# Order of the max units and the value product inside a step of the unmasked attentions of a two-layer decoder

## The chip, the cores and the metric

The kernel runs on one core of one Trainium2 chip. The metric is the device time in microseconds (us) of one execution; lower is better. The core has five engines with instruction streams of their own, which meet only at semaphores: TensorE (PE in the profile, its weight loads PEld), VectorE (DVE), ScalarE (ACT), GpSimd (POOL) and SyncE (SP, which issues DMAs here).

## The reference: what is computed

The input is 2048 tokens of 256 features, with a context of 1601 tokens. Two decoder layers follow one another. Each has a causal self-attention, a cross-attention to the context, and a feed-forward part, each followed by a layer norm. There are thus four attentions of 16 heads of 16 features each:

1. layer 0, self-attention, causal (2048 x 2048 scores a head), with rotary positions;
2. layer 0, cross-attention with a mask on the keys (2048 x 1601);
3. layer 1, self-attention, causal;
4. layer 1, cross-attention without a mask (2048 x 1601).

Each computes `softmax(q k^T / 4) v` for every head, then a product with an output matrix. The last part of layer 1 is a mixture of eight experts with a shared one.

## The kernel before, in words

All four attentions are built by one function, `attention_phase` (L103). A **head** is worked off in **steps**, which are listed in `slots`: a step is one tile of 128 keys (`kt`) against one half (1024) of the queries. Cross-attention has 26 steps a head (13 key tiles, two halves). Causal attention has 24 (16 key tiles; the first half of the queries has no part in key tiles 8 to 15, and the further down the diagonal, the fewer the columns). The last field of a slot says whether it is the second half of its key tile, which is where the product with the values stands.

Scores are computed transposed (keys in the rows of PSUM, queries in its columns), and ACT takes their exponential. So the maximum of each query has to be known before, and it is got from a second computation of the same scores, the other way round: the **units** (`unit`, PE at L541, DVE at L725). One unit is 128 queries against up to 512 keys. PE makes it with four matmuls side by side (L555), each in a quarter of the array's columns and in one half of its rows: `g % 2` picks the half for unit number g. It writes one of **three** PSUM banks (`M_BANKS = 3`), bank `g % 3`. DVE reads the bank and reduces it to 128 maxima: `tensor_reduce` (L747) for whole units, a fused add and maximum with the triangular mask (L734) for a unit that ends on the diagonal, and in attention 4 one reduction over four narrow units at once (L745). The PE's wait ahead of a unit is the one that matters here:

```python
                    if g >= M_BANKS:
                        pe.wait_ge(unit_used, g - M_BANKS + 1)
```

Unit g may thus be issued only when DVE has finished unit g - 3. A causal head has 40 units, the cross-attention of layer 1 has 52 (four of them of 4 x 65 columns).

The other kinds of PE work in a step are:

- `scores(h, n)` (L559): the scores of slot n with the maxima already subtracted. There are two PSUM areas for them (`S_PS`), so it waits until ACT has finished the slot two before. The columns of the first bank use the lower half of the array's rows, those of the second bank the upper half. L576 is its matmul; in attention 1 a crossing of the diagonal adds four short ones (L582).
- `product(h, n)` (L599): probabilities of one key tile times the values, for all queries, only in steps of the second half. Its matmuls (L616) are float32 and use all 128 rows of the array. It waits for the exponentials of slot n (and in attention 3 for a selection on POOL, L439).

ACT makes one exponential a step (L480) of up to 1024 columns, and once a head copies the output out (L453).

The units of head h + 1 (for late steps those of head h + 2) are spread over the steps of head h in proportion to the step's columns: `share[n]` and `before[n]`. A step gets 0 to 3 units in a causal head and exactly 2 in attention 4. The loop at L668 to L684 then writes PE's order by hand. For step n it is: scores of step n + 2; the first half of the step's units (rounded up); in attention 2 alone the mask products; the value product if the step has one; and the rest of the units. Nothing else in the kernel sets the order of these. DVE takes the units in the same order 0, 1, 2, ... whatever stands between them, with the five small steps of `finish_max` (L749) between the first units of a head.

Of the kernel before, what the change touches and what calls it, by code (L numbers as in the profile page):

```python
# [102 lines left out]
def attention_phase(nc, e, keys, causal, masked, loads, query, key, value, ahead, projection, normed, eps, kept=None,  # L103
# [12 lines left out]
    slots = []  # L116
# [9 lines left out]
    for t in range(NT):  # L126
        cut = tiles((t + 1) * P, CH) if causal else tiles(keys, -(-keys // -(-keys // CH)))
        if wide and t % 4 == 0:
            units += [(t + j, i, a, CH, False, 1) for j in range(4) for i, (a, _) in enumerate(tiles(keys, CH)[:-1])]
            units.append((t, keys // CH, keys // CH * CH, keys % CH, False, 4))  # L130
        elif not wide:
            units += [(t, i, a, w, causal and a + w == (t + 1) * P, 1) for i, (a, w) in enumerate(cut)]
# [28 lines left out]
    with ExitStack() as held, phase(nc) as sem:  # L161
# [91 lines left out]
        with nc.Block() as block:  # L253
# [255 lines left out]
            def _(pe):  # L509
# [31 lines left out]
                def unit(h, u):  # L541


                    t, piece, a, w, diagonal, count = units[u]
                    g, b = h * nu + u, h % 3
                    if u == 0:
                        pe.wait_ge(stack_in[b], 192 * (h // 3 + 1))
                    if g >= M_BANKS:
                        pe.wait_ge(unit_used, g - M_BANKS + 1)
                    bank, first = e.ps[:, g % M_BANKS, :], g % 2 * ROWS  # L550
                    rows = slice(first, first + KQ)
                    for i in range(count):
                        for j in range(4):
                            at = (t + i) * P + 32 * j
                            last = nc.tensor.matmul(bank[quarter(j), i * w:i * w + w], qs[b][rows, at:at + 32],  # L555
                                                    ks[b][rows, a:a + w], start=True, stop=True)
                    last.then_inc(unit_ready, 1)

                def scores(h, n):  # L559

                    kt, rows, half, first, diagonal, _ = slots[n]
                    diagonal = diagonal and not select
                    g, b = h * ns + n, h % 3
                    if n == 0:
                        pe.wait_ge(max_in, 32 * (h + 1))
                    if g >= 2:
                        pe.wait_ge(exp_done, g - 1)
                    groups = -(-rows // 32)
                    for bank in range(2):
                        lo, hi = max(first, bank * CH), (bank + 1) * CH  # L570
                        if lo >= hi:
                            continue
                        crossed = diagonal and lo == first
                        at = bank * ROWS
                        for j in range(groups):
                            last = nc.tensor.matmul(S_PS(g)[quarter(j), lo:hi], ks[b][at:at + KM, kt * P + 32 * j:kt * P + 32 * j + 32],  # L576
                                                    qs[b][at:at + KM, half * HALF + lo:half * HALF + hi],
                                                    start=True, stop=not (crossed or masked))
                        if crossed:
                            for j in range(groups):  # L580
                                own = at + 32 * (j % 2)
                                last = nc.tensor.matmul(S_PS(g)[quarter(j), lo:lo + P], e.ident16[at:at + ROWS, own:own + 32],  # L582
                                                        e.lower16[at:at + ROWS, j // 2, :], start=False, stop=True)
                    if not masked:
                        last.then_inc(s_ready, 1)

                def mask_scores(h, n):

                    kt, rows, half, first, diagonal, _ = slots[n]
                    g = h * ns + n  # L590
                    for bank in range(2):
                        lo, hi = bank * CH, (bank + 1) * CH
                        for j in range(-(-rows // 32)):
                            last = nc.tensor.matmul(S_PS(g)[quarter(j), lo:hi], e.big16[0:rows, quarter(j)],  # L594
                                                    e.mask_one[0:rows, kt, half * HALF + lo:half * HALF + hi],
                                                    start=False, stop=True)
                    last.then_inc(s_ready, 1)

                def product(h, n):  # L599

                    kt, rows, _, _, _, _ = slots[n]
                    tile = h * nk + kt
                    pe.wait_ge(exp_done, h * ns + n + 1)
                    if select:
                        pe.wait_ge(selected, tile + 1)
                    if kt == 0 and h:
                        pe.wait_ge(o_copied, h)
                    if tile == 0 and v_bias:
                        pe.wait_ge(v_shifted, nk)
                    weights = e.prob[tile % P_SLOTS].rearrange("p (b j q) -> p b j q", j=4, q=P)  # L610
                    for j in range(4):
                        b0 = max(0, -(-(kt - j) // 4)) if causal else 0
                        if b0 == 4:
                            continue
                        end = kt == (12 + j if causal else nk - 1)
                        last = nc.tensor.matmul(O_PS[quarter(j, HD + 1), b0 * P:CH], e.values[0:rows, kt, h, :],  # L616
                                                weights[0:rows, b0:4, j, :], start=(kt == 0), stop=end)
                    last.then_inc(pv_done, 1)
# [49 lines left out]
                for h in range(H):  # L668
                    for n in range(ns):
                        if n + 2 < ns:  # L670
                            scores(h, n + 2)
                        elif h + 1 < H:
                            scores(h + 1, n + 2 - ns)
                        turned = h + (1 if n <= turn else 2)
                        now = range(before[n], share[n]) if turned < H else range(0)
                        middle = -(-len(now) // 2)
                        for u in now[:middle]:
                            unit(turned, u)
                        if masked and h * ns + n + 2 < H * ns:
                            mask_scores(h + (n + 2) // ns, (n + 2) % ns)  # L680
                        if slots[n][5]:
                            product(h, n)
                        for u in now[middle:]:
                            unit(turned, u)  # L684
# [1604 lines left out]
```

## Time and profile before

| | |
|---|---|
| median of 3 runs | 2954.4 us (2951.17 to 2958.16) |
| the profiled execution, its own time | 2952.49 us |
| span in its trace | 2950.7 us |
| mean granted TensorE clock | 0.963 of full speed |
| PE busy | 2762.6 us (94%) |
| DVE busy | 2153.8 us (73%) |
| ACT busy | 1821.0 us (62%) |
| POOL busy | 544.2 us (18%) |

The span runs from the first to the last instruction; 1.8 us of the profiled execution lie around it. In the span, the steps of attention 1 run from about 142 to 533 us, those of attention 2 (masked) from about 634 to 1292, those of attention 3 from about 1453 to 1840, and those of attention 4 from about 2063 to 2579; the stretches between are projections, norms and feed-forward parts, and the experts stand at the end. Matmuls are pipelined, so a PE that is shown as busy need not be at its peak, and the recorded length of a matmul is longer than the time until the next one in the same place can start.

### The profile page before, as it was taken

How to read it: one execution, taken by the hardware profiler on the slowest of the kernel's cores; microseconds unless marked ns; L12 is line 12 of the kernel's file. 1: busy time of each engine (PE TensorE's matmuls, PEld its weight loads, DVE VectorE, ACT ScalarE, POOL GpSimd, SP SyncE). 2: the span in 40 equal slices, each digit the busy share in tenths (PEclk: the TensorE clock that was granted, in tenths of full speed). 3: DMA queues.
4: the chain of work that ended last, by engine and by line, in shares of the span. 5: the costliest groups of instructions: out<-in, count | busy, mean ns of one | idle time of the engine just before them, and what ended most of it. 6: DMA issues, size and time to landing. Idle time of an engine off the chain costs nothing. (4 is left out here: it accounts for less than half of the span.)

```text
span 2950.7 us, 93752 instructions
## 1 busy us (share of the span) xinstructions
PE 2762.6 (94%) x39186; PEld 1026.9 (35%) x39187; DVE 2153.8 (73%) x5870; ACT 1821.0 (62%) x2158; POOL 544.2 (18%) x760
## 2 busy tenths in 40 slices
PE   4999999999999999985999999999999999999997
PEld 2633332522222222232322222563222222266664
DVE  7699997488888888837799996327999999561115
ACT  2278888537777777763388888322888888922222
POOL 0188880120000000001222212301100000002330
PEclk7899999979999999996899999998999999999999
DMA  3345451311000110110211112202112221121112
GB/s 98 118 116 139 128 127 48 113 29 26 26 17 24 26 27 22 24 26 31 79 41 42 42 43 50 67 2 85 26 54 54 75 60 34 36 71 58 44 43 88
DMA packets 120405, 166.78 MB, mean 57 GB/s; under 512 B 38227, under 2 KB 89310, under 8 KB 119984
## 3 DMA queue, kind: packets, MB, share of 16 engines
q1 hardware_dynamic: 102192, 117.21, 14.8%
q0 software_dynamic: 12320, 43.02, 4.8%
q8 instruction: 310, 5.08, 0.7%
q10 hardware_dynamic: 5472, 0.56, 0.2%
q14 instruction: 111, 0.91, 0.1%
HBM read 126.51 MB, written 26.72 MB: 52 GB/s over the span
## 5 line engine op out<-in xcount | busy, mean ns | idle before, releaser
L747 DVE TENSOR_REDUCE mpart<-ps 128x1 f32<-128x512 f32 x1536 | 979.1, 684 | 77.9 <-PE ps L555 74.5
L555 PE MATMUL ps<-stack 48*32 48x512 f16 (+6 forms) x13312 | 947.4, 350 | 39.5 <-DVE mpart L747 13.6
L480 ACT ACTIVATE xT<-ps,exp_scale 128x1024 f32<-128x1024 f32 (+3 forms) x800 | 794.1, 1029 | 256.4 <-PE ps L594 122.9
L480 ACT ACTIVATE cn<-ps,exp_scale 128x1024 f32<-128x1024 f32 (+4 forms) x800 | 742.2, 960 | 193.6 <-PE ps L594 92.7
L576 PE MATMUL ps<-stack 50*32 50x512 f16 (+3 forms) x11648 | 747.7, 372 | 29.4 <-ACT xT L480 22.1
L555 PEld LDWEIGHTS ps<-stack 48*32 48x32 f16 x13312 | 281.9, 90 | 1018.1 <-DVE mpart L747 515.0
L740 DVE CUSTOM_DVE_ANT_0 scrap<-ps,arena 128x401 bf16<-128x401 f32 (+1 forms) x1024 | 533.8, 574 | 121.8 <-PE ps L555 121.8
L616 PE MATMUL ps<-xT,vall 128*17 128x512 f32 (+4 forms) x3648 | 411.0, 511 | 2.7 <-POOL xT L439 1.7
L616 PE MATMUL ps<-cn,vall 128*17 128x512 f32 (+3 forms) x3392 | 406.3, 500 | 1.3 <-ACT cn L480 1.0
L734 DVE CUSTOM_DVE_ANT_0 scrap<-ps,scrap 128x128 bf16<-128x128 f32 (+3 forms) x512 | 247.3, 484 | 14.9 <-PE ps L555 9.8
L594 PE MATMUL ps<-arena,big 128*32 128x512 fp8e4 (+1 forms) x3264 | 256.7, 386 | 0.0
L576 PEld LDWEIGHTS ps<-stack 50*32 50x32 f16 x11648 | 186.5, 89 | 175.9 <-ACT xT L480 94.2
L1681 PE MATMUL ps<-arena,vall 128*128 x312 | 146.6, 593 | 0.6 <-ACT vall L1755 0.6
L1938 DVE TENSOR_TENSOR vall<-osb,ps 128x512 f32<-128x512 f32 x39 | 26.8, 688 | 146.0 <-PE ps L1681 146.0
L1771 ACT ACTIVATE osb<-ps 128x512 f32<-128x512 f32 x39 | 23.3, 598 | 169.8 <-PE ps L1681 169.8
L1162 POOL PARTITION_ALL_REDUCE small<-small x1 | 0.4, 373 | 679.5 <-issue 679.5
L616 PEld LDWEIGHTS ps<-cn,vall 128*17 128x17 f32 (+1 forms) x3392 | 70.0, 96 | 108.5 <-issue 67.7
L616 PEld LDWEIGHTS ps<-xT,vall 128*17 128x17 f32 (+1 forms) x3648 | 71.1, 96 | 104.6 <-issue 52.9
L427 POOL TENSOR_SCALAR arena<-wbuf 128x401 bf16<-128x401 int32 x64 | 101.3, 1583 | 7.2 <-DMA wbuf<-in_mask 3.5
L1584 POOL IOTA vall<- 128x16 f32 x1 | 0.2, 153 | 531.1 <-POOLq L253 531.1
L594 PEld LDWEIGHTS ps<-arena,big 128*32 128x32 bf16 (+1 forms) x3264 | 50.1, 94 | 118.4 <-issue 118.4
L740 DVE DVE_READ_ACCUMULATOR2_ANT mpart<- 128x1 f32 x1024 | 85.1, 83 | 0.0
(282 smaller groups left out, 2547.0 us busy)
## 6 DMA issues: line engine op xcount, KB each, us to landing
stack<-q_parts SPq DMA_DIRECT2D x384, 64.0 KB, 3.3
stack<-k_parts SPq DMA_DIRECT2D x192, 64.0 KB, 3.2
wbuf<-in_maskT POOLq DMA_DIRECT2D x24, 512.0 KB, 4.8
arena<-in_moe_w SPq DMA_DIRECT2D x19, 512.0 KB, 4.5
stack<-k_parts SPq DMA_DIRECT2D x192, 50.0 KB
stack<-sums_inverse SPq DMA_DIRECT2D x16, 512.0 KB, 6.1
parts<-osb SPq DMA_DIRECT2D x240, 32.0 KB
wbuf<-in_mask POOLq DMA_DIRECT2D x16, 401.0 KB, 4.1
```

What stands on the lines that cost most here:

```text
L427: chain.link(nc.gpsimd.tensor_scalar(e.mask_add[:, t, a:a + n], stage.bitcast(I32), 0.0, MASKED, ALU.is_equal, ALU.mult))
L480: nc.scalar.activation(e.prob[tile % P_SLOTS][0:rows, half * HALF + first:(half + 1) * HALF], S_PS(g)[0:rows, first:HALF], ACT.Exp, scale= ...
L555: last = nc.tensor.matmul(bank[quarter(j), i * w:i * w + w], qs[b][rows, at:at + 32], ks[b][rows, a:a + w], start=True, stop=True)
L576: last = nc.tensor.matmul(S_PS(g)[quarter(j), lo:hi], ks[b][at:at + KM, kt * P + 32 * j:kt * P + 32 * j + 32], qs[b][at:at + KM, half * HA ...
L594: last = nc.tensor.matmul(S_PS(g)[quarter(j), lo:hi], e.big16[0:rows, quarter(j)], e.mask_one[0:rows, kt, half * HALF + lo:half * HALF + h ...
L616: last = nc.tensor.matmul(O_PS[quarter(j, HD + 1), b0 * P:CH], e.values[0:rows, kt, h, :], weights[0:rows, b0:4, j, :], start=(kt == 0), s ...
L734: nc.vector.tensor_tensor_reduce(out=e.scrap[:, t % 3, 0:w], in0=src, in1=e.scrap[:, 3, CH - w:CH], scale=1.0, scalar=-3.0e38, op0=ALU.add ...
L740: nc.vector.tensor_tensor_reduce(out=e.scrap[:, g % 4, 0:w], in0=src, in1=e.mask_add[:, t, a:a + w], scale=1.0, scalar=-3.0e38, op0=ALU.ad ...
L747: nc.vector.tensor_reduce(dst, src, AX, ALU.max).then_inc(unit_used, 1)
L1681: last = nc.tensor.matmul(bank, e.pair_xT[i % 2][:, c, :], w, start=(c == 0), stop=(c == NC - 1))
L1771: nc.scalar.activation(e.gated_s[i % 2], a_bank(i), ACT.Silu).then_inc(pair_silu, 1)
L1938: nc.vector.tensor_tensor(e.pair_h[i % 2], e.gated_s[i % 2], b_bank(i), ALU.mult).then_inc(pair_h, 1)
```

## The change

In the loop that writes PE's order, the number of units that stand ahead of the value product is no longer half (rounded up) but all of them, in steps that have a product (`slots[n][5]`) and in attentions without a mask (1, 3 and 4). Steps without a product write their units one after another in either version. The masked attention 2 is unchanged. No instruction is added or removed on any engine, no wait, no DMA and no buffer is changed.

```diff
@@ -673,7 +673,7 @@
                             scores(h + 1, n + 2 - ns)
                         turned = h + (1 if n <= turn else 2)
                         now = range(before[n], share[n]) if turned < H else range(0)
-                        middle = -(-len(now) // 2)
+                        middle = len(now) if slots[n][5] and not masked else -(-len(now) // 2)
                         for u in now[:middle]:
                             unit(turned, u)
                         if masked and h * ns + n + 2 < H * ns:
```

## Rows read from the trace of the kernel before

**Rows 1.** The page: span, and busy time of each engine.
```profile
span 2950.7 us, 93752 instructions
PE 2762.6 (94%) x39186; PEld 1026.9 (35%) x39187; DVE 2153.8 (73%) x5870; ACT 1821.0 (62%) x2158; POOL 544.2 (18%) x760
```

**Rows 2.** Busy time by stretch: PE, PEld, DVE, ACT, POOL, then PEclk, DMA share, GB/s.
```profile
143.00:570.00 427.00, 409.05 (x7883) 139.59 (x7872) 357.83 (x967) 337.41 (x429) 261.66 (x247) 0.99 0.40 108
1460.00:1825.00 365.00, 349.10 (x6488) 97.79 (x6480) 325.01 (x891) 302.12 (x377) 83.68 (x257) 0.99 0.17 41
2037.00:2071.00 34.00, 31.88 (x312) 6.77 (x312) 30.85 (x59) 4.94 (x5) 5.70 (x9) 0.51 0.09 23
2071.00:2580.00 509.00, 480.08 (x8586) 115.32 (x8583) 465.52 (x839) 440.56 (x429) 5.32 (x8) 1.00 0.19 49
```

**Rows 3.** Waits in attention 4 (2071 to 2580): total us, times, longest.
```profile
PEld ps L555 <- DVE mpart L747: 298.4, 479, 1.3
...
ACT cn L480 <- PE ps L576: 34.1, 80, 2.0
ACT xT L480 <- PE ps L576: 33.2, 83, 0.8
PEld ps L555 <- DVE mpart L745: 17.8, 43, 0.9
...
DVE mpart L747 <- PE ps L555: 11.4, 44, 0.7
```

**Rows 4.** PE in order of time, two steps of attention 4: start, us, line, shape, count.
```profile
2308.30 0.40 PE L555 MATMUL ps<-stack 48*32 48x512 f16 x4
2308.62 1.05 PE L616 MATMUL ps<-xT,vall 128*17 128x512 f32 x8
2309.61 0.40 PE L555 MATMUL ps<-stack 48*32 48x512 f16 x4
2309.62 0.60 PE L576 MATMUL ps<-stack 50*32 50x512 f16 x8
2309.84 0.64 PE L555 MATMUL ps<-stack 48*32 48x512 f16 x8
2310.11 0.60 PE L576 MATMUL ps<-stack 50*32 50x512 f16 x8
2310.80 0.40 PE L555 MATMUL ps<-stack 48*32 48x512 f16 x4
2311.13 1.05 PE L616 MATMUL ps<-xT,vall 128*17 128x512 f32 x8
2312.11 0.40 PE L555 MATMUL ps<-stack 48*32 48x512 f16 x4
```

**Rows 5.** DVE in order of time, the same two steps.
```profile
2310.05 0.69 DVE L747 TENSOR_REDUCE mpart<-ps 128x1 f32<-128x512 f32 x1
2310.66 0.68 DVE L747 TENSOR_REDUCE mpart<-ps 128x1 f32<-128x512 f32 x1
2311.26 0.68 DVE L747 TENSOR_REDUCE mpart<-ps 128x1 f32<-128x512 f32 x1
2311.86 0.68 DVE L747 TENSOR_REDUCE mpart<-ps 128x1 f32<-128x512 f32 x1
2312.56 0.69 DVE L747 TENSOR_REDUCE mpart<-ps 128x1 f32<-128x512 f32 x1
```

**Rows 6.** ACT in order of time, the same two steps.
```profile
2307.77 2.12 ACT L480 ACTIVATE xT<-ps,exp_scale 128x1024 f32<-128x1024 f32 x2 [0.29 <-PE ps L576]
2310.27 2.12 ACT L480 ACTIVATE cn<-ps,exp_scale 128x1024 f32<-128x1024 f32 x2 [0.38 <-PE ps L576]
```

**Rows 7.** PE in order of time, steps 3 to 5 of a head of attention 1.
```profile
297.07 0.40 PE L555 MATMUL ps<-stack 48*32 48x512 f16 x4
297.40 1.05 PE L616 MATMUL ps<-xT,vall 128*17 128x384 f32 x8
298.38 0.24 PE L555 MATMUL ps<-stack 48*32 48x128 f16 x4
298.40 0.44 PE L576 MATMUL ps<-stack 50*32 50x128 f16 x8
298.46 0.23 PE L582 MATMUL ps<-lower,ident 64*32 64x128 bf16 x4
298.52 0.75 PE L555 MATMUL ps<-stack 48*32 48x512 f16 x8
298.89 0.60 PE L576 MATMUL ps<-stack 50*32 50x512 f16 x8
299.11 0.39 PE L555 MATMUL ps<-stack 48*32 48x512 f16 x4
299.43 0.62 PE L616 MATMUL ps<-cn,vall 128*17 128x384 f32 x4
```

**Rows 8.** DVE groups of attention 1, shapes apart: count, busy us, mean ns.
```profile
L747 DVE TENSOR_REDUCE mpart<-ps 128x1 f32<-128x512 f32 x351 | 227.5, 683 | 25.8 <-PE ps L555 25.4
L734 DVE CUSTOM_DVE_ANT_0 scrap<-ps,scrap 128x512 bf16<-128x512 f32 x58 | 39.7, 685 | 3.6 <-PE ps L555 1.4
L734 DVE CUSTOM_DVE_ANT_0 scrap<-ps,scrap 128x384 bf16<-128x384 f32 x58 | 31.9, 551 | 0.0
L734 DVE CUSTOM_DVE_ANT_0 scrap<-ps,scrap 128x256 bf16<-128x256 f32 x57 | 23.9, 420 | 2.9 <-PE ps L555 2.6 <-issue 0.2
L734 DVE CUSTOM_DVE_ANT_0 scrap<-ps,scrap 128x128 bf16<-128x128 f32 x57 | 16.0, 281 | 0.0
```

**Rows 9.** Waits in attention 1 (143 to 570): total us, times, longest.
```profile
PEld ps L555 <- DVE mpart L747: 79.6, 137, 1.7
PEld ps L555 <- DVE mpart L734: 57.4, 126, 0.6
...
PEld ps L576 <- ACT xT L480: 33.0, 70, 1.9
```

**Rows 10.** The page: one group of the products, with the idle time ahead of it.
```profile
L616 PE MATMUL ps<-xT,vall 128*17 128x512 f32 (+4 forms) x3648 | 411.0, 511 | 2.7 <-POOL xT L439 1.7
```

**Rows 11.** PE in order of time, a product of attention 4 at the lower clock.
```profile
2067.26 1.91 PE L616 MATMUL ps<-xT,vall 128*17 128x512 f32 x8
2069.10 0.61 PE L555 MATMUL ps<-stack 48*32 48x512 f16 x4
...
2071.06 0.80 PE L616 MATMUL ps<-xT,vall 128*17 128x512 f32 x4
```

## The prediction

> **What bounds the kernel now.** I read the page first, then the busy time by stretch, the waits of a stretch, and at last two steps in order of time. By the page, PE is busy 94% of the span and DVE 73% [rows 1], which points to PE; that is an average over stages, and a busy PE need not be at its peak. In attention 4 DVE is busy 465.5 us of 509 and PE 480.1 [rows 2]: both nearly full, so neither alone explains the time. The waits tell more: PE's weight loads for units waited 479 times for a DVE reduction, 298.4 us in all, while DVE waited for a unit only 11.4 us [rows 3]. Most of the 298 us is nothing lost (a weight load cannot start while a product runs anyway), so the chain has to be followed by the clock.
>
> Rows 4 to 6 are two steps of attention 4. Call the four units of such a pair A (behind the product), B, C, D (ahead of it). The order is P A S B | C S D P, with S the scores, P the product. Times: P starts at 2308.62, A at 2309.61, S 2309.62, B 2309.84, C and S 2310.09 to 2310.11, D at 2310.80, P at 2311.13, the next A at 2312.11 [rows 4]. Why does D stand so late? It needs the bank of A. DVE starts on A at 2310.05 and takes 0.69 [rows 5], done at 2310.74; D starts 0.06 later. So the chain that sets the pace is a ring:
>
> - A starts, DVE starts on it: 0.45 later (2312.11 to 2312.56, where DVE's start is 0.70 behind the one before instead of 0.60, so it did stand idle) [rows 4, 5]
> - DVE on A 0.69, then 0.06 until D starts
> - D to P 0.33 (2310.80 to 2311.13), P to the next A 0.98 [rows 4]
>
> Sum 0.45 + 0.69 + 0.06 + 0.33 + 0.98 = 2.51, and P to P is 2.51 [rows 4]. The ring closes. The limits beside it: four reductions at 0.60 from start to start are 2.40 [rows 5], two exponentials 2.12 with 0.38 idle [rows 6]. The product lies in the ring, and while it runs (0.98) DVE lives on what the three banks hold.
>
> **The change, part by part.** Nothing is added or removed. Only A moves: it now stands ahead of the product, as fourth unit, and the order is P S A' B' | S C' D' P. On PE it passes one product; it passes no DMA, and no wait of SP or POOL is touched. Behind the product stands now S.
>
> (a) Attention 4. What D' needs is the bank of A', three units ahead, as before. But A' is now behind P **and** behind the first half of S. A' uses the lower half of the array's rows, and so do the scores of the first bank. So A' starts as B does today behind S: 0.22 after the start of S (2309.62 to 2309.84) [rows 4]. I put S at P's end plus nothing, A' at plus 0.22. Ring: 0.98 + 0.22 + 0.45 + 0.69 + 0.06 + 0.33 = 2.73 against 2.51, **+0.22 a pair**. Does DVE reach A' late instead, which would hide it? D' starts at T; DVE began on B' just before, so B', C', D' at 0.60 end at about T + 1.8; A' is ready at T + 0.33 + 0.98 + 0.22 + 0.45 = T + 1.98. DVE has run dry; nothing hides it. Where a pair holds the unit of 4 x 65 columns, the ring is shorter in one order or the other; I closed the ring interval by interval over the 13 of a head and get +0.21 in seven of them and +0.57, +0.32, +0.18, +0.11, -0.01 and -0.15 in the six that have to do with a narrow unit, which stands at another place of the ring in the other order: +2.5 us a head. Units are made in 15 heads; the first and the last have a little less. **+37 us.**
>
> (b) Attention 1. Here 11 units a head are moved (steps 1, 3, 5 and so on to 15, and 16 to 18). The same ring, with other lengths: today the unit behind P is often the one that ends on the diagonal, short on PE and on DVE (281, 420, 551 ns at 128, 256, 384 columns against 683) [rows 8]. So the ring through it is short: P to P is 2.03 (297.40 to 299.43) with a 128-column unit behind P [rows 7]. After the change that unit stands fourth, where its length counts little, and the first behind S is a whole one: 0.98 + 0.10 (S and its crossing of 128 columns) + 0.45 + 0.68 + 0.06 + 0.22 (a 256-column unit to P) = 2.49, +0.47. Interval by interval through a head, P to P from step 1 on: 0, +0.47, +0.32, +0.19, +0.06, -0.22, +0.14, +0.11, +0.13, then 0 where a step has one unit or none, and +0.47 over the head's border. Sum **+1.66 a head, 15 heads: +25 us.** The gains and zeros are where exponentials or PE set the pace (scores waited for ACT 33 us in the stage, units for DVE 137 us) [rows 9].
>
> (c) Attention 3, other shares: -0.08, -0.11, +0.36, +0.32, -0.08, +0.19, -0.08, +0.32, -0.08, then 0, border +0.60: **+1.36 a head, +20 us.** That the product comes later than the selection on POOL gains nothing: in the whole kernel these products waited 1.7 us for POOL [rows 10].
>
> (d) Attention 2 and the rest: unchanged, 0. The heads' maxima are placed by DMA after the last unit of a head; units move earlier within their step only, but all shift with the ring, so that chain keeps its slack.
>
> Sum 37 + 25 + 20 = 82, less rounding **81 us**. The profiled execution is 2952.5, so 3033.5; the median of the runs is 1.9 above it: I say 3034.
>
> **What is not shown.** No row has S right behind P with two units behind it. The lag of A' is bounded by 0.01 (a unit beside scores on the other half, 2309.61 and 2309.62) and 0.22 [rows 4]; I take 0.22 in attention 4, where the halves are the same in every pair, and the crossing's 0.10 in attention 1. With 0.01 in attention 4 that term falls to nothing: 2952.5 + 44 = 2997. At the other end each of 13 + 11 + 11 moved units in 15 heads pays 0.22: 525 x 0.22 = 116, giving 3068.
>
> **The rivals.**
>
> - *Hidden in the causal attentions.* There PE waits less for DVE (137 us against 316) and DVE has more room (358 of 427 busy) [rows 2, 3, 9]. If PE's own time sets the pace there, only (a) is paid: 2989. Against it: the 2.03 of rows 7 closes only through the banks.
> - *Faster.* The scores no longer stand behind a unit that needs a bank and, in half of the steps, the same rows of the array; ACT gets them up to 0.21 sooner, and it waits for scores 67 us in attention 4 [rows 3]. If ACT closed the interval, some 165 of the 330 causal steps would gain 0.21: 35 us, 2918. It decides once two exponentials (2.12) exceed the bank ring (2.51 today); they don't [rows 4, 6].
> - *Nothing.* If the lag were hidden by other slack everywhere: 2954.
> - *Clock.* In attention 4 the granted clock is 1.00 (2.4 GHz) over 509 us, though the ring leaves PE short idle times; before 2071 it was 0.51 (1.2 GHz for most of it), behind projections in which PE waited [rows 2]. At the lower level P to P was 3.80 (2067.26 to 2071.06) [rows 11]: 1.3 x 195 pairs is 250 us, 3290 with the rest. The Trainium skill (TensorE: Matmul & The Clock Gate, A second HAM failure mode) says that micro-idling between matmul groups while cycling through PSUM banks can make the clock oscillate; that speaks against this change, which adds such idling. By that rule the time would be the rival's; the trace, which cycles three banks with idle gaps at full clock, does not bear it out.
>
> **How the numbers follow.** A measurement can tell about 0.2% (6 us) here. Forecast (3034, own range 3012 to 3056) 0.88; causal part hidden 0.06; clock 0.02; nothing 0.02; faster 0.02. Slower: 0.88 + 0.06 + 0.02 = 0.96; same 0.02; faster 0.02. The range 3010 to 3058 leaves out the rivals and the outer ends of the bounds.
>
> **What would show it.** Right: in attention 4 P to P goes from 2.51 to about 2.73, the first unit behind P starts some 0.22 after the scores, DVE's wait for units (11.4 us) rises to some 50 to 60 us, and DVE's busy time stays. Attention 1 grows by 25, attention 3 by 20, attention 2 by nothing. Wrong: if A' starts beside S, if DVE shows no more idle time, or if P to P in steps 3 to 7 of a causal head stays near 2.1. A granted clock below 1.00 inside 2071 to 2600 would be the clock rival.

## The result, and the profile after

The changed kernel takes 3046.99 us (median of 4 runs, 3045.45 to 3048.54) against 2953.95 us before: ratio 1.0316, 95% interval 1.0304 to 1.0329. It is 93 us slower. The profiled execution takes 3046.02 us, its span is 3044.2. The forecast was 3034 in a range of 3010 to 3058.

The page of the changed kernel, span and busy time of each engine, and two of its groups:

```profile
span 3044.2 us, 93753 instructions
...
PE 2772.9 (91%) x39187; PEld 1041.6 (34%) x39187; DVE 2164.1 (71%) x5870; ACT 1821.7 (60%) x2158; POOL 544.4 (18%) x760
...
L747 DVE TENSOR_REDUCE mpart<-ps 128x1 f32<-128x512 f32 x1536 | 979.9, 683 | 144.8 <-PE ps L555 141.6
L555 PE MATMUL ps<-stack 48*32 48x512 f16 (+6 forms) x13312 | 920.1, 349 | 122.3 <-DVE mpart L747 111.8
```

The same two groups on the page of the kernel before:

```profile
L747 DVE TENSOR_REDUCE mpart<-ps 128x1 f32<-128x512 f32 x1536 | 979.1, 684 | 77.9 <-PE ps L555 74.5
L555 PE MATMUL ps<-stack 48*32 48x512 f16 (+6 forms) x13312 | 947.4, 350 | 39.5 <-DVE mpart L747 13.6
```

The engines do the same work as in [rows 1]: DVE 2164 us busy against 2154, ACT 1822 against 1821. The 93 us are waiting. Both sides of the hand-over between the units on PE and their reductions on DVE wait for each other more than they did: DVE stands idle 144.8 us ahead of L747 (77.9 before), PE 122.3 us ahead of L555 (39.5 before). A pair in which each of two engines waits for the other and neither is full points to a ring through both.

The busy time by stretch (columns as in [rows 2]):

```profile
143.00:600.00 457.00, 418.36 (x7872) 142.57 (x7873) 361.05 (x967) 336.50 (x430) 261.38 (x248) 0.98 0.38 101
1485.00:1870.00 385.00, 353.13 (x6431) 98.06 (x6426) 332.23 (x895) 298.83 (x371) 81.14 (x253) 0.97 0.16 38
2122.00:2632.00 510.00, 444.50 (x8152) 117.68 (x8148) 459.39 (x826) 405.02 (x391) 5.24 (x8) 0.99 0.17 47
```

In attention 4, 510 us now hold 444.5 us of PE and 405.0 of ACT, where 509 us held 480.1 and 440.6 [rows 2]. From the first scores of an attention to its last:

| | before | after | difference | forecast |
|---|---|---|---|---|
| attention 1 | 389.3 | 418.0 | +28.7 | +25 |
| attention 2 | 657.1 | 657.6 | +0.5 | 0 |
| attention 3 | 386.9 | 410.3 | +23.5 | +20 |
| attention 4 | 513.0 | 552.3 | +39.3 | +37 |

Sum 92.0; the remaining 1.5 of the 93.5 us of span lie between the attentions. The median head of attention 1 went from 24.36 to 26.29 us, of attention 3 from 24.08 to 25.46, of attention 4 from 32.49 to 35.00.

Two pairs of steps of attention 4, PE in order of time:

```profile
2336.45 0.41 PE L576 MATMUL ps<-stack 50*32 50x512 f16 x8
2336.68 0.40 PE L555 MATMUL ps<-stack 48*32 48x512 f16 x8
2336.89 0.40 PE L576 MATMUL ps<-stack 50*32 50x512 f16 x8
2337.11 0.39 PE L555 MATMUL ps<-stack 48*32 48x512 f16 x4
2337.86 0.40 PE L555 MATMUL ps<-stack 48*32 48x512 f16 x4 [0.36 <-DVE mpart L747]
2338.19 1.05 PE L616 MATMUL ps<-xT,vall 128*17 128x512 f32 x8
2339.17 0.41 PE L576 MATMUL ps<-stack 50*32 50x512 f16 x8
2339.40 0.40 PE L555 MATMUL ps<-stack 48*32 48x512 f16 x8
2339.62 0.40 PE L576 MATMUL ps<-stack 50*32 50x512 f16 x8
2339.84 0.39 PE L555 MATMUL ps<-stack 48*32 48x512 f16 x4
2340.58 0.40 PE L555 MATMUL ps<-stack 48*32 48x512 f16 x4 [0.36 <-DVE mpart L747]
2340.91 0.62 PE L616 MATMUL ps<-xT,vall 128*17 128x512 f32 x4
```

and the reduction with which DVE takes up the first unit behind a product:

```profile
2337.11 0.69 DVE L747 TENSOR_REDUCE mpart<-ps 128x1 f32<-128x512 f32 x1 [0.50 <-PE ps L555]
```

Read against [rows 4]: behind the product (2338.19) come both halves of the scores at once, 2339.17, and the two units 0.23 later. DVE starts on the first of such a pair 0.43 later (2336.68 to 2337.11), behind 0.50 us of idle time that [rows 5] do not have; it is done at 2337.80 and the fourth unit starts at 2337.86. P to P is 2.72 (2338.19 to 2340.91) against 2.51, where 2.73 was forecast.

The waits of attention 4, as in [rows 3]:

```profile
PEld ps L555 <- DVE mpart L747: 144.9, 190, 0.9
PEld ps L576 <- ACT cn L480: 69.7, 81, 1.7
PEld ps L576 <- ACT xT L480: 67.2, 79, 0.9
PE ps L555 <- DVE mpart L747: 62.9, 174, 0.5
ACT cn L480 <- PE ps L576: 51.8, 86, 2.0
ACT xT L480 <- PE ps L576: 50.9, 88, 1.8
DVE mpart L747 <- PE ps L555: 48.0, 153, 1.7
```

and two lines of the kernel before, one of its waits in attention 4 and the weight loads of the unit behind the product of 2308.62:

```profile
PE ps L555 <- DVE mpart L747: 7.2, 29, 0.8
...
2309.60 0.10 PEld L555 LDWEIGHTS ps<-stack 48*32 48x32 f16 x4 [0.85 <-DVE mpart L747]
```

DVE's wait for units rose from 11.4 to 48.0 us. The wait of the units' weight loads fell from 298.4 to 144.9 although the kernel got slower. Much of that number is time under a running product: the 0.85 us ahead of 2309.60 all lie inside the product that started at 2308.62. In the changed order the first weight loads behind a product are those of the scores (L576), and such waits stand in their rows now, 136.9 us where there were 22.6. The line in which PE's matmuls themselves waited for DVE is the one that shows idle PE: 62.9 us, where there were 7.2.

### The profile page after: what moved, and what is told of

The parts are those of the page before. It is cut to its first block and busy times, and to the rows that moved or that the text cites. A ratio compares the mean times of both kernels' runs of the same rounds, so it can differ in the third digit from the quotient of the medians.

```text
span 3044.2 us, 93753 instructions
## 1 busy us (share of the span) xinstructions
PE 2772.9 (91%) x39187; PEld 1041.6 (34%) x39187; DVE 2164.1 (71%) x5870; ACT 1821.7 (60%) x2158; POOL 544.4 (18%) x760
## 5 line engine op out<-in xcount | busy, mean ns | idle before, releaser
L747 DVE TENSOR_REDUCE mpart<-ps 128x1 f32<-128x512 f32 x1536 | 979.9, 683 | 144.8 <-PE ps L555 141.6
L555 PE MATMUL ps<-stack 48*32 48x512 f16 (+6 forms) x13312 | 920.1, 349 | 122.3 <-DVE mpart L747 111.8
L576 PE MATMUL ps<-stack 50*32 50x512 f16 (+3 forms) x11648 | 684.0, 373 | 28.7 <-ACT xT L480 22.9
L740 DVE CUSTOM_DVE_ANT_0 scrap<-ps,arena 128x401 bf16<-128x401 f32 (+1 forms) x1024 | 533.7, 573 | 122.3 <-PE ps L555 122.3
L555 PEld LDWEIGHTS ps<-stack 48*32 48x32 f16 x13312 | 276.5, 91 | 725.6 <-DVE mpart L740 317.8
L576 PEld LDWEIGHTS ps<-stack 50*32 50x32 f16 x11648 | 186.6, 90 | 556.5 <-ACT xT L480 258.6
```

Of the source, the lines that this page charges most:

```text
L740: nc.vector.tensor_tensor_reduce(out=e.scrap[:, g % 4, 0:w], in0=src, in1=e.mask_add[:, t, a:a + w], scale=1.0, scalar=-3.0e38, op0=ALU.ad ...
L747: nc.vector.tensor_reduce(dst, src, AX, ALU.max).then_inc(unit_used, 1)
```

## The experiments

**Which attentions pay, and do they add up?** The change in attention 4 alone (`wide` is true there only):

```diff
-                        middle = -(-len(now) // 2)
+                        middle = len(now) if slots[n][5] and wide else -(-len(now) // 2)
```

> The change in attention 4 alone. Ring theory (unit, VectorE, fourth unit, product, scores): P to P goes from 2.51 to 2.73 us, attention 4 grows by 37 us, and attentions 1 and 3 stay at 24.36 and 24.08 us a head; total about 2991, and up to 2996 if the granted clock falls for short stretches inside attention 4 as it did twice with the whole change. Rival (the clock makes up most of the loss): without the dips nothing is lost, total below 2970. If the three parts interact (what one loses another gives back), the sum of this run's loss and that of the run with attentions 1 and 3 alone differs from 93 us by more than 10.

Measured: 2994.75 us (median of 4 runs), ratio 1.0141 (1.0125 to 1.0156). A median head of attention 4 takes 34.99 us, attentions 1 and 3 keep 24.37 and 24.09. The profile has one stretch at the lower clock in attention 4 (3.4 us from 2527.4), so the clock is not what costs the 40 us; that rival is out.

And the same with `causal` in place of `wide`:

> The change in the two causal attentions alone. Ring theory: a head of attention 1 takes 26.0 to 26.3 us (24.36 before), a head of attention 3 25.45 (24.08 before), total 2954 + 45 to 54 = 2999 to 3008; attention 4 stays at 32.49 a head. Rival (hidden in the causal attentions, since PE's own time sets their pace): total within 10 us of 2954.

Measured: 3004.83 us (median of 4 runs), ratio 1.0174 (1.0158 to 1.0189). Heads of attention 1 take 26.29 us, of attention 3 25.45; attention 4 keeps 32.49. The two ratios add to 1.0315, the whole change has 1.0316. In medians (the kernel before took 2955.1 beside these runs) the parts cost 39.7 and 49.7, together 89.4 of 93. The parts do not touch each other, as far as these 4 us can tell, and the rival of a loss hidden in the causal attentions is out.

**What is in the ring: the scores?** In the order of before, half of the columns of those scores that stand behind the product are left out:

```diff
                         lo, hi = max(first, bank * CH), (bank + 1) * CH
                         if lo >= hi:
                             continue
+                        if wide and half == 0:
+                            hi = lo + CH // 2
```

> The order of before; in attention 4 the scores of the first half of the queries (those that stand right behind the unit behind the product) are computed for 256 of the 512 columns of each bank only, the rest of each bank is left as it is; that part of the scores is left out. Ring theory: these scores are not in the ring of the old order, so attention 4 keeps 2.51 us from product to product and 32.5 a head, total 2954 within 3. Rival (TensorE's own time or its packing sets the pace): 0.11 less for each of 190 pairs, 21 us less, 2933.

Measured: one run, 2957.8 us, against 2949.1 for the kernel before beside it. The median head of attention 4 takes 32.49 us, to the hundredth what it took with all the columns. The products in order of time:

```profile
2280.33 1.05 PE L618 MATMUL ps<-cn,vall 128*17 128x512 f32 x8
2282.84 1.05 PE L618 MATMUL ps<-xT,vall 128*17 128x512 f32 x8
2285.34 1.05 PE L618 MATMUL ps<-xT,vall 128*17 128x512 f32 x8
```

They are 2.51 and 2.50 apart. PE work was taken away in each pair and no time was won in the stage. The total was not within the 3 us expected: this run shows two stretches of 3.4 us at a granted clock of 0.50, in attentions 3 and 4, and slower first heads; from one run I take the median heads and not the total.

The same lines in the changed order:

> The changed order with the same part of the scores left out in attention 4. Ring theory: in the new order these scores stand between the product and the first unit, their 0.22 becomes 0.11, P to P 2.73 becomes 2.62, attention 4 shortens by about 20 us (a head from 35.0 to 33.6), total about 3027. If the scores in the gap had nothing to do with the loss (a theory in which the loss comes from the two units in a row ahead of the product): no difference, 3047.

Measured: one run, 3031.8 us. The median head of attention 4 takes 33.70 us against 35.00, which is 0.10 for each of its 13 pairs. The products:

```profile
2389.43 1.05 PE L618 MATMUL ps<-cn,vall 128*17 128x512 f32 x8
2392.04 1.05 PE L618 MATMUL ps<-cn,vall 65*17 65x512 f32 x8
2394.65 1.05 PE L618 MATMUL ps<-xT,vall 128*17 128x512 f32 x8
```

They are 2.61 apart, where 2.62 was expected. The same scores are free in the old order and paid in the new. That the loss came from two units in a row ahead of the product is out.

**What is in the ring: how many reductions?** DVE reads half of each bank in attention 4, so half of each unit's maxima is left out; PE's work is the same.

```diff
-                        nc.vector.tensor_reduce(dst, src, AX, ALU.max).then_inc(unit_used, 1)
+                        part = src[:, 0:CH // 2] if wide else src
+                        nc.vector.tensor_reduce(dst, part, AX, ALU.max).then_inc(unit_used, 1)
```

In the changed order:

> The changed order; in attention 4 VectorE reduces only 256 of the 512 columns of a unit (half of each maximum is left out), TensorE's work is the same. Ring theory: one reduction is in the ring, 0.68 becomes about 0.42, P to P 2.73 becomes 2.47, 34.8 to about 31.8 a head. Rival (VectorE's throughput): four reductions count, 1.04 less, and P to P drops to what ScalarE needs, about 2.2. Rival (TensorE's own time): 2.73 stays.

Measured: one run, 2982.2 us, 31.78 us a head. The group of reductions, and two products in order of time:

```profile
L748 DVE TENSOR_REDUCE mpart<-ps 128x1 f32<-128x256 f32 x566 | 206.2, 416 | 136.9 <-PE ps L555 136.7
```

```profile
2300.45 1.05 PE L616 MATMUL ps<-cn,vall 128*17 128x512 f32 x8
...
2302.91 1.05 PE L616 MATMUL ps<-cn,vall 128*17 128x512 f32 x8
```

One reduction fell from 683 to 416 ns, by 0.27 us, and P to P from 2.72 to 2.46, by 0.26. Four reductions fell by 1.07. So one of the four is in the ring, and DVE's throughput is not what sets the pace in this order.

In the order of before:

> The order of before with the same half reductions in attention 4. Ring theory: 2.51 becomes 2.25, and the new order is still 0.22 dearer, that is some 37 us in attention 4 with VectorE far from full (about 1.7 of 2.25 us). Rival (the new order costs time because VectorE is full): with half reductions both orders take the same time.

Measured: one run, 2889.2 us, 29.05 us a head, and from product to product 2.24:

```profile
2250.69 1.05 PE L616 MATMUL ps<-cn,vall 128*17 128x512 f32 x8
...
2252.93 1.05 PE L616 MATMUL ps<-xT,vall 128*17 128x512 f32 x8
```

With half reductions the new order costs 31.78 - 29.05 = 2.73 us a head, with DVE busy 225 (new) and 239 (old) of 375 us (2125 to 2500); with whole reductions, where DVE is nearly full in the old order, it costs 2.51. The loss is one of order. A full DVE isn't needed for it. In this run ACT comes close to being the limit (359.6 us busy of the same 375), but the ring still closes: the unit behind the product of 2250.69 starts at 2251.68, DVE takes it up at 2252.13, the fourth unit starts at 2252.61 and the product at 2252.93.

**Can the ring be made shorter?** First the opposite move: in steps without a product a unit goes ahead of the scores (the lines that compute `turned` and `now` move up for it, which is left out here).

```diff
...
+                        if not masked and not slots[n][5] and now:
+                            unit(turned, now[0])
+                            now = now[1:]
                         if n + 2 < ns:
                             scores(h, n + 2)
```

> The kernel before, with one more unit moved the other way: in steps without a product (attentions 1, 3, 4) the first unit stands ahead of the scores instead of behind them. Ring theory: in attention 4 the ring does not change (P A, then B ahead of S instead of behind: 2.51), and in the causal attentions where a unit beside scores reaches VectorE a little sooner 2 to 3 us each are won: 2954 - 5 = 2949. Rival (scores that come later starve ScalarE): 0.2 us in each of some 7 causal and 13 cross steps a head, 2954 + 20 or more.

Measured: 2945.35 us (median of 9 runs), ratio 0.9969 (0.9959 to 0.9979), a little faster than the kernel before and clear of the noise. Attention 4 keeps 32.50 us a head, as its ring says. Attention 1 takes 385.1 us in all (389.3 before) and attention 3 382.9 (386.9): 8 us, where 5 were expected. The rival, a starving ScalarE, is out.

Then the product itself, the longest member of the ring (0.98 of 2.51). On top of the edit before, in attention 4, key tiles 1 to 11, it is cut by queries into halves, with two units and the scores between them; the first and the last tile stay whole because their matmuls open and close the accumulation.

```diff
...
+                        split = wide and slots[n][5] and 0 < slots[n][0] < nk - 1
+                        if split:
+                            product(h, n, 0)
+                        if now and not masked and (split or not slots[n][5]):
+                            unit(turned, now[0])
+                            now = now[1:]
                         if n + 2 < ns:
                             scores(h, n + 2)
...
-                        middle = -(-len(now) // 2)
+                        middle = len(now) if split else -(-len(now) // 2)
...
-                            product(h, n)
+                            product(h, n, 1 if split else None)
```

and in `product`, which takes `half=None` as a third argument:

```diff
-                        last = nc.tensor.matmul(O_PS[quarter(j, HD + 1), b0 * P:CH], e.values[0:rows, kt, h, :],
-                                                weights[0:rows, b0:4, j, :], start=(kt == 0), stop=end)
-                    last.then_inc(pv_done, 1)
+                        b1 = 4
+                        if half is not None:
+                            b0, b1 = 2 * half, 2 * half + 2
+                        last = nc.tensor.matmul(O_PS[quarter(j, HD + 1), b0 * P:b1 * P], e.values[0:rows, kt, h, :],
+                                                weights[0:rows, b0:b1, j, :], start=(kt == 0), stop=end)
+                    if half != 0:
+                        last.then_inc(pv_done, 1)
```

> As the run with the unit ahead of the scores, and in attention 4 the product of key tiles 1 to 11 is cut into two halves of 256 queries, the first at the head of the step, the second at its end, with two units and the scores between. Ring theory: VectorE is fed in the middle of what was one block of 0.98 us, so the ring through the product is no longer the longest one and P to P falls from 2.51 to between 2.2 and 2.4 (VectorE's own four reductions are 2.40): attention 4 is 19 to 20 us shorter, the total 2954 - 19 - 5 = 2930. Rival (TensorE's own time sets the pace in attention 4): twice as many products, some 0.24 more per pair of steps for filling and emptying the array: 165 pairs x 0.24 = 40 us more, 2994.

Measured: 2935.41 us (median of 5 runs), ratio 0.9937 (0.9923 to 0.9950), the fastest version here that computes everything. Attention 4 takes 500.5 us in place of 513.0, 31.42 a head. PE in order of time, first halves at 2319.97 and 2322.39:

```profile
2319.97 0.63 PE L619 MATMUL ps<-cn,vall 128*17 128x256 f32 x8
2320.53 0.40 PE L555 MATMUL ps<-stack 48*32 48x512 f16 x4
2320.55 0.59 PE L576 MATMUL ps<-stack 50*32 50x512 f16 x8
2320.78 0.39 PE L555 MATMUL ps<-stack 48*32 48x512 f16 x4
2321.27 0.63 PE L619 MATMUL ps<-cn,vall 128*17 128x256 f32 x8
...
2322.39 0.63 PE L619 MATMUL ps<-cn,vall 128*17 128x256 f32 x8
```

and DVE over the same time:

```profile
2319.38 5.46 DVE L757 TENSOR_REDUCE mpart<-ps 128x1 f32<-128x512 f32 x9
```

Nine reductions in one piece without a gap: 5.46 us, 0.60 from start to start (the last one's 0.68 counted whole), 2.4 for four. DVE is busy 370.0 of 375 us (2125 to 2500). The ring is no longer the longest; DVE's own work is, and no order of PE's work alone goes below it: the interval is 31.42 / 13 = 2.42. TensorE's own time as the bound is out for these heads: it did more and the stage got shorter. I expected 19 to 20 us from attention 4 and got 12.5. The 15 heads beside which units are made gained 15.1 together, since I had let some intervals close below DVE's own four reductions. The last head, beside which no units are made, lost 2.2: its P to P, 2.01 before, is 2.21 with the split. Where DVE does not set the pace, the split product is paid for.

## Why the prediction was right, point by point

- **The ring of five members** (0.45 + 0.69 + 0.06 + 0.33 + 0.98). Shown. Taking 0.27 off a reduction shortens P to P by 0.26 to 0.27 in either order, and the scores count in the new order alone.
- **(a) Attention 4, lag of the first unit 0.22, +0.22 a pair, +2.5 a head.** P to P 2.72 against 2.50 in most intervals (medians), +2.51 a head. For the six intervals with a narrow unit, forecast +0.57, +0.32, +0.18, +0.11, -0.01 and -0.15, the medians give +0.56, +0.31, +0.22, +0.13, -0.08 and -0.17. The stage grew by 39.3 where 37 was forecast; two short stretches at the lower clock (below) hold 2.9 of it, and without them it is 36.4.
- **(b) Attention 1, +1.66 a head.** Right in kind, 0.27 a head too small: +1.93. The medians of the intervals, before and after, are 2.51 and 2.51, 2.03 and 2.51, 2.14 and 2.57, 2.33 and 2.57, 1.69 and 1.75, 1.79 and 1.57, 1.64 and 1.74, 1.39 and 1.48, 1.17 and 1.45, no difference in the next, and 2.20 and 2.68 over the border. The mis-sized terms are the third, the fourth and the ninth: I had +0.32, +0.19 and +0.13, measured are +0.43, +0.24 and +0.28. The third had no working in the prediction. Its ring closes at 2.56 in the trace, with a unit of 384 columns as the fourth: product at 312.62, scores 0.98 later, DVE 0.56 behind them, the fourth unit 0.75 later and the product after 0.27, at 315.18. What makes up the fourth and the ninth was not taken apart. Four us of the 12 missing ones are this.
- **(c) Attention 3, +1.36 a head.** +1.38 in the median head. The stage grew by 23.5 in place of 20; four stretches at the lower clock hold 4.9 of it, and without them it is 18.6, a little under the forecast.
- **(d) Attention 2 and the rest.** +0.5 and +1.5 us.
- **The sum.** By heads the three terms are 37.5 + 24.9 + 20.4 = 82.8; the "less rounding 81" has no reason behind it and is 1 to 2 us low.
- **DVE's wait for units 50 to 60 us.** 48.0, a little under.
- **The clock rival, 0.02.** It was not the likeliest and not the size I gave it, but it was not nothing either. The sign set for it, a granted clock below 1.00 inside the stage of attention 4, did come, but as 6.8 us in all and not as 250 us. The granted clock was not lost over a stage; it fell to 0.50 (1.2 GHz) six times for 3.4 us each, four times in attention 3 and twice in attention 4; the profile of the kernel before has none in either. These are the two in attention 4, and the stretch at 1.00 between them:

```profile
2224.50:2227.90 3.40, 3.35 (x48) 0.88 (x52) 1.78 (x3) 1.65 (x3) 0.00 (x0) 0.51 0.32 95
2227.90:2296.20 68.30, 59.28 (x1096) 15.63 (x1084) 61.84 (x112) 54.60 (x53) 0.00 (x0) 1.00 0.19 55
2296.20:2299.60 3.40, 3.40 (x52) 0.79 (x48) 1.79 (x4) 1.77 (x3) 0.00 (x0) 0.50 0.32 82
```

  Within the first one a product takes its lower-clock time (from its start to the scores behind it 1.84, as in [rows 11], against 0.98):

```profile
2225.09 1.91 PE L616 MATMUL ps<-cn,vall 128*17 128x512 f32 x8
2226.93 0.63 PE L576 MATMUL ps<-stack 50*32 50x512 f16 x8
```

  A head with such a stretch takes 1.2 to 1.5 us more (attention 3: 26.66, 26.76 and 26.61 against 25.46, and 27.37 against 26.13 for the same head in the run with attentions 1 and 3 alone; attention 4: 36.49 and 36.37 against 35.00), so six make about 8 us, most of what the forecast lacked beside term (b). The Trainium skill (TensorE: Matmul & The Clock Gate, A second HAM failure mode), whose rule I weighed and set aside, says that small idle times between matmul groups, while PSUM banks are cycled, make the clock go back and forth between its two levels. The trace agrees in kind, with six falls worth 0.3% of the time; that the idle times set them off is not shown by any run here.

The mechanism was thus right, and so were the sizes of its terms but for those three intervals. The forecast was 13 us low: 4 us in attention 1 and 8 us of clock were missed, 4 us more are the rounding, attention 2 and the stretches between, and the unrounded ring terms of attentions 3 and 4 were 3 us too high. That these errors partly cancel is luck.

The faster rival was wrong where I said it would be: the ring was the longest, so scores that come sooner give nothing. ACT's waits for scores in attention 4 rose from 67 to 103 us.

## What to carry to other kernels

Where two engines wait for each other and both look nearly full, add up the ring, from one fill of a buffer to the next: the start of the fill (here a unit on PE), its drain (the reduction on DVE), the release, the fill that needs the buffer, and whatever PE does before it comes back to the start. An item costs time only if it stands in that ring; the same scores were free in one order and 0.22 us a pair in the other. To make such a kernel faster, order the work so that what the draining engine waits for stands directly behind the longest block, or cut that block (here 0.98 us of product) so that the drain is fed in its middle. The cut is paid for wherever the drain does not set the pace, as in the last head here.

## What the runs showed of the hardware that was not expected

Short falls of the granted clock inside a busy stage, in places that mostly come back: in three runs with the new order in attention 3 they began at 1539.7, 1693.3 and 1771.8 us, at 1540.5, 1694.1 and 1772.6, and at 1541.2, 1694.8 and 1773.3; in the fourth, the changed kernel itself, at 1538.5, 1743.3, 1770.6 and 1797.9. Over all ten profiles, attention 3 had 13 such stretches in the four with the new order and 2 in the six with the old one; attention 4 had 2, 1, 4 and 0 in the four profiles with the new order, and one in the six others. Of the four with the new order in attention 4, the one without any is that with half reductions, whose PE is busy 96% of the middle of the stage, as in the kernel before (95%); in the changed kernel and in the run with the shorter scores, which had 2 and 4, it is 87%. That fits idle time on PE as the cause, but with one profile of each kernel it is no proof: what sets them off was not tried and stays open.
